# A PSUM bank changed for the last front piece of a step, in a kernel of patch tokens, linear attention and experts

## The reference

```
h = tok(x)                      # 4 shifted copies of x beside x, layer norm over the image, gamma, beta,
                                # convolution with 8x8 patches: 169 tokens of 128 features per image
h = h + attn(layernorm(h))      # 8 heads: q' = exp(q proj), k' = exp(k proj),
                                # out = q' (k'^T v) / (q' sum(k') + 1e-6), then the output matrix
h = h + ffn(layernorm(h))       # 8 experts, the 2 best of each token by a gate, silu(xW) * (xV) W2
```

## Time and profile before

| | |
|---|---|
| median of the three runs | 1154.52 us |
| the profiled execution | 1159.75 us |
| its span, first to last instruction | 1158.0 us (1.75 us lie around it) |
| mean granted clock of TensorE | 0.983 of full speed |
| TensorE busy | 1088.3 us, 94% |
| VectorE busy | 882.1 us, 76% |
| ScalarE busy | 561.7 us, 49% |
| GpSimd busy | 613.2 us, 53% |

### The profile page before, as it was taken

How to read it: one execution, slowest core, us unless ns; L and a number is a source line. 1 busy time by engine, 2 the same in 40 slices (tenths; PEclk the granted TensorE clock), 3 DMA queues, 4 the chain that set the end, 5 groups by cost and what they waited for, 6 DMA issues and landing times.

```text
span 1158.0 us, 29957 instructions
## 1 busy us (share of the span) xinstructions
PE 1088.3 (94%) x8580; PEld 924.0 (80%) x8581; DVE 882.1 (76%) x3333; ACT 561.7 (49%) x1307; POOL 613.2 (53%) x656
## 2 busy tenths in 40 slices
PE   3899999999999999999999669999999999999995
PEld 3667777777777777777776468999999999999995
DVE  5468887888888878878867567777777777777774
ACT  3444535436355354363343424555555555555552
POOL 0103444445444454454444456586767676677675
PEclk9899999999999999999999979999999999999998
DMA  8270131301311313111010324343434343343442
GB/s 166 47 200 21 32 78 29 81 29 33 78 33 36 74 32 79 30 32 32 30 34 28 104 69 73 47 57 54 55 53 55 52 57 51 53 57 53 54 55 30
DMA packets 76011, 65.51 MB, mean 57 GB/s; under 512 B 12338, under 2 KB 66802, under 8 KB 75926
## 3 DMA queue, kind: packets, MB, share of 16 engines
q0 software_dynamic: 32704, 24.99, 15.2%
q1 hardware_dynamic: 43078, 39.16, 14.0%
q10 hardware_dynamic: 144, 0.32, 0.1%
HBM read 32.72 MB, written 31.71 MB: 56 GB/s over the span
## 4 chain that ended last, share of the span: by engine, by line
PE 79%; DVE 9%; SPq 4%; issue 3%; DMA 3%; ACT 1%; POOL 0%; POOLq 0%; DVEq 0%; ACTq 0%
PE bank L1440 21%; PE bank L1457 13%; PE bank L677 6%; PE bank L612 5%; PE bank L726 5%; PE bank L739 4%; PE bank L713 4%; PE bank L715 3%; PE bank L714 3%; PE bank L732 3%; DVE patches L824 2%; PE bank L605 2%; PE bank L476 2%; PE bank L1428 2%; DMA out_rows<-yo,dest 2%
## 5 line engine op out<-in xcount | busy, mean ns | idle before, releaser
L1612 POOL DMA_INDIRECT out_rows<-yo,dest x184 | 312.4, 1698 | 140.4 <-issue 107.0
L1440 PE MATMUL bank<-xT_e,wv 128*128 128x256 f32 x2208 | 291.9, 288 | 5.4 <-DVE xT_e L1546 3.5
L1440 PEld LDWEIGHTS bank<-xT_e,wv 128*128 128x128 f32 x2208 | 273.9, 191 | 6.1 <-DVE xT_e L1546 4.0
L1323 POOL DMA_INDIRECT sorted_rows<-xrow_all,sloti x192 | 191.4, 997 | 88.4 <-issue 52.8
L1516 ACT ACTIVATE sil<-bank 128x256 f32<-128x256 f32 x368 | 141.1, 384 | 173.0 <-PE bank L1440 152.3
L1457 PE MATMUL bank<-w,hid 128*128 x1472 | 182.0, 277 | 3.0 <-DVE hid L1553 3.0
L1457 PEld LDWEIGHTS bank<-w,hid 128*128 128x128 f32 x1472 | 173.6, 194 | 4.4 <-issue 4.4
L1553 DVE TENSOR_TENSOR hid<-sil,bank 128x256 f32<-128x256 f32 x368 | 143.9, 417 | 24.8 <-ACT sil L1516 20.9
L1535 DVE TENSOR_TENSOR wv<-wv_all,wv 128x1024 fp32r<-128x1024 f32 x92 | 113.3, 1232 | 64.4 <-PE bank L1440 48.8
L1234 ACT ACTIVATE attn<-bank 128x256 f32<-128x256 f32 x128 | 49.4, 386 | 162.1 <-issue 127.1
L1498 ACT CAST wv<-wv_all 128x1024 fp32r x92 | 96.1, 1046 | 29.4 <-issue 27.9
(11 more groups left out here) (213 smaller groups left out, 1802.8 us busy)
## 6 DMA issues: line engine op xcount, KB each, us to landing
xr<-sorted_rows SPq DMA_DIRECT2D x92, 130.0 KB
raw<-in_x SPq DMA_DIRECT2D x64, 84.5 KB
raw<-in_x SPq DMA_DIRECT2D x60, 78.0 KB
out_rows<-attn SPq DMA_DIRECT2D x64, 58.5 KB
sorted_rows<-xrow_all,sloti POOLq DMA_INDIRECT x192
out_rows<-yo,dest POOLq DMA_INDIRECT x184
wv_all<-in_L_ffn_W SPq DMA_DIRECT2D x8, 256.0 KB, 6.0
wv_all<-in_L_ffn_V SPq DMA_DIRECT2D x8, 256.0 KB, 6.2
```

Of the source, the lines that this page charges most:

```text
L1323: po.indirect_dma_start(sorted_rows, bass.IndirectOffsetOnAxis(sloti[:, p, j, ch:ch + 1], 0), xrow[:, p, j, ch], None).then_inc(s(f"scatte ...
L1440: q = pe.matmul(bank[fc][:, TT * m:TT * m + TT], wv[:, w, w_, m, cols], xT[:, p, x_], start=(w_ + x_ == 0), stop=(w_ == 1))
L1612: po.indirect_dma_start(out, bass.IndirectOffsetOnAxis(dest[:, p, a:a + 1], 0), yo[:, p, a], None, compute_op=ALU.add).then_inc(s(f"added{ ...
```

## The change

The piece at the fourth place of a step goes through bank 3 in place of bank 0. On TensorE it waits for `xT_low` of this step, so that bank 3 is free; and since it no longer shares a bank with the piece ahead of it, `ahead` = 1 takes one from the count of `front_evac` for which it waits. VectorE reads it from bank 3. No instruction moves on any engine. The transposes and multiplications are the same, and each first transpose of a fourth-place piece has one more semaphore to wait for (four in place of three).

```diff
                 def front(i):
+
                     if fr and k in TURN and TURN[k][i] is not None:
-                        front_piece(g + 1, TURN[k][i])
+                        if i == 3:
+                            pe.wait_ge(s("xT_low"), n + 1)
+                            front_piece(g + 1, TURN[k][i], 3, 1)
+                        else:
+                            front_piece(g + 1, TURN[k][i])
...
                     if fr and k in TURN and TURN[k][i] is not None:
                         if TURN[k][i] == 0:
                             at_least(ve, s("conv_done"), 4 * g)
-                        front_piece(g + 1, TURN[k][i], 1 - par)
+                        front_piece(g + 1, TURN[k][i], 1 - par, 3 if i == 3 else 0)
```

## The result

| | kernel before | changed kernel |
|---|---|---|
| median | 1154.62 us (22 runs, 1151.43 to 1157.37) | 1151.63 us (22 runs, 1150.01 to 1158.2) |
| ratio, 95% interval | | 0.9979 [0.9970, 0.9988] |
| the profiled execution, its span | 1159.75, 1158.0 us | 1150.36, 1148.6 us |

The change makes the kernel 0.21% faster, 2.4 us by the ratio and 3.0 us by the medians. The forecast was 1151.0 us. Timed again in another session, the same change gave 0.9969 [0.9951, 0.9988].

The account below looks back on a forecast made before the run. TensorE was taken as nearly the bound (94% busy), with VectorE bounding some stretches. Gains of 2.4 + 0.55 + 0.6 = 3.55 us from a 1154.5 us median gave 1151.0 us, range 1148.8 to 1154.2.

Parts of the forecast that it names:

- Which wait ends last: Behind the fourth-place piece, which engine ends the next wait: gain 0.40 us in six k = 1 steps, 0.55 first k = 2.
- Later steps k = 2, TensorE's side: Six later k = 2 steps: VectorE is back to back, so TensorE's 0.55 us returns as idle time; gain 0.
- The casts: VectorE's four casts beside GpSimd's scatter, later k = 2: between 0.22 gain and 0.06 loss, taken as 0.1 us, six times.
- The page's rule: Casts beside the scatter: whichever starts first keeps the shared port pair its whole instruction; in full, 1156.0 us.
- the slower rival: Later k = 2 steps: scatters hold the first and fourth casts, losing 0.74 us in each of six; 1156.0 us, chance 0.05.
- New costs: Added `xT_low` wait at 14 pieces: at most 0.3 us, taken as 0; ACT copy ahead of L739's second half: none.
- All paid: Rival: TensorE is the bound everywhere, so all 6.25 us of removed waits is gained; about 1148 us, chance 0.08.
- Nothing paid: Rival: every removed wait comes back ahead of L558 and L637, at k = 1 as well; 1154.5 us, chance 0.15.
- The chances: Whole kernel: faster by over 0.2% 0.68, within 0.2% 0.27, slower 0.05; the forecast case itself 0.68.

Follow-up runs that it names:

- the two halves: The change made only at steps k = 1 (k1_only) or only at steps k = 2 (k2_only), against the kernel before; ratios 0.9968 and 0.9991.
- bank_only: Bank 3 as in the change, but TensorE still waits until the piece ahead is read, against the kernel before; ratio 1.0013, steps 0.1 us less.
- k2_only: Only the fourth-place piece of steps k = 2 goes through bank 3, against the kernel before; ratio 0.9991, steps 1.3 us less.
- k1_only: Only the fourth-place piece of steps k = 1 goes through bank 3, against the kernel before; ratio 0.9968, steps 2.5 us less.
- late_scatter: Whole change, and GpSimd's first scatter of each step waits for VectorE's reciprocal, against the kernel before; ratio 0.9936, steps 5.9 us less.

## Why the prediction was right, and where it was not

**Which wait ends last.** Right. The prediction divided the 13 removed waits by what VectorE does behind them, and the trace and the two halves follow this division: 0.37 to 0.40 us in each of six steps k = 1 (0.40 forecast), 0.52 in the first step k = 2 (0.55 forecast), and a small rest in the six later ones. Of the 6.25 us that TensorE got back at the piece, 3.8 reached the end of the steps. The rest is 0.4 us per later step k = 2 between L610 and L642.

**Later steps k = 2, TensorE's side.** Wrong in size: 0 forecast, 0.12 to 0.15 us measured in five of the six, 0.7 us together, and 0.3 in the one whose wait had been 0.66. The prediction read "VectorE is back to back" from L902 starting at 161.19, 0.02 us after piece 3's end. But VectorE's rows overlap when nothing is waited for: L891 starts at 157.43 in front of the end of L824 at 157.51; I had that row's end and did not use it.

```profile
157.43 0.85 DVE L891 TENSOR_SCALAR xrow_all<-attn,mv,rstd 128x128 f32<-128x128 f32 x3
```

In the changed kernel L907 starts 0.08 us ahead of piece 3's end. So L902 had been waiting for L605 for 0.1 us. The rows at hand said so in another way too: L902 starts 0.07 us behind the end of L605 both at k = 1, where it plainly waits for it (141.76 to 141.83), and at k = 2 (161.12 to 161.19).

**The casts.** The bounds held, the value in the middle did not. Forecast a gain between 0.22 and a loss of 0.06, taken as 0.1; measured, a loss of 0.02 (1.05 to 1.07 us): the third cast is free and the first is held. The scatter itself came about where it was put, 0.38 us behind the denominator with 0.43 forecast. So the six later steps were to give 0.6 us, all of it by the casts, and gave 1.0, none of it by them. That the sum of 3.55 us came out near 3.8 in the steps, with one term too small and one too large, is luck in part. So is the time: 1151.0 us forecast and 1151.6 measured are closer than the kernel can be told by, since its 22 runs differ by 6 us, and by the ratio the gain was 2.4 us and not 3.55.

**The page's rule.** The Trainium skill, page "SBUF — State Buffer", section "Who interferes with whom", has the first to start hold the shared port pair for its whole instruction. The first cast, from 161.16 on, ended with the scatter (160.55 + 1.06 = 161.61), so a hold by the scatter is what happens. It is not for the whole instruction: before, two casts ran undisturbed inside the scatter's 1.06 us and the third was held; and the fourth cast behind k = 2 was not caught by the second scatter (161.92). So the slower rival failed at its second half. The second cast before, at 162.41, began 0.63 us ahead of the scatter's end and was free. Two other steps bring the border closer. The third cast in step n = 4 of the kernel before began 0.48 us ahead of the end (105.81) and was free, and the first cast in step n = 23 of the changed one began 0.47 us ahead (467.40) and was held:

```profile
104.72 1.09 POOL L1323 DMA_INDIRECT sorted_rows<-xrow_all,sloti  x1 [0.72 <-issue]
```

```profile
105.33 0.20 DVE L916 CAST rparts<-rden 32x86 fp32r<-32x86 f32 x1
```

```profile
466.34 1.06 POOL L1328 DMA_INDIRECT sorted_rows<-xrow_all,sloti  x1 [0.72 <-issue]
```

```profile
466.93 0.46 DVE L921 CAST rparts<-rden 32x84 fp32r<-32x84 f32 x1
```

**New costs.** None, as forecast: bank_only holds both and differs by 0.1 us from before. The ACT copy L1234, on which the second half of L744 waits, ended in time; TensorE's rows there show no idle time.

**The rivals.** All paid: out by k2_only. Nothing paid: out by k1_only. **The chances** were right in that the change was clear of no change (interval below 1), though the first ratio, 0.21%, lies at the edge of the 0.2% that I wanted told from none, and its interval reaches from 0.12% to 0.30%.

## What to carry to other kernels

A removed wait is worth what the next common point lets through. Go from the wait to the place where the other engine takes over, and look at that engine's idle time there: it paid all of the 0.39 us where the idle time was 0.71, and 0.13 of 0.55 where it was almost nothing. On an engine whose rows overlap by 0.08 us when it runs free, a gap of 0.02 us is a wait of 0.1. Where the other engine has become the bound, move its work, here a lighter piece and a later scatter: they gave 2.4 and 2.1 to 2.6 us beside the 3.8 of the bank, and the lighter piece gave it only with the bank changed. And look at the clock of each stretch before a difference of two whole spans is put down to a change.

## What the runs showed of the hardware that I had not expected

- An indirect DMA on GpSimd (1.06 us) holds up VectorE's casts from float32 to fp32r only near its end: those that began 0.47 us or less ahead of it lasted until it was over, and those that began 0.48 us or more ahead were not held. The border is read from four of the profiles. Starting it 1.0 us later, behind the reciprocal, frees all casts: 0.82 or 0.83 us for the four in every step, in place of 0.89 to 1.06 beside a scatter, 1.05 in most.
- In some of otherwise equal steps an engine goes on about 0.4 us late with nothing in the rows to wait for: ScalarE behind a TensorE product (late_scatter, 6.29 in place of 5.90 us behind L907), or VectorE behind its own instruction (0.46 us idle ahead of L833, in the step n = 22 of all twelve profiles). The cause is open.
- The spread of the executions goes with TensorE's granted clock, which is 1.00 in the steps but not in the set-up, behind step n = 30 and in the first 50 us of the expert part. Those 50 us had 0.88 in the three profiles with the longest expert part (477.3 to 477.4 us) and 0.91 to 0.97 in the other nine (472.6 to 476.0). Of the last session's 17 executions of the kernel before, the five with a mean clock of 0.980 or 0.981 took 1160.2 us on average, the seven with 0.985 to 0.988 took 1154.6.
